# Retention and MoE layer on eight cores: which PSUM banks hold the hoisted LayerNorm sums, and how the GroupNorm broadcasts take turns on theirs

## What is computed

```python
# retention, on xn = layernorm(x)
q, k, v = xh @ wq, xh @ wk, xh @ wv            # per head, 16 heads of 64
scores = einsum('bsnd,btnd->bnst', q, k) * D   # D: causal decay gamma_n^(s-t)
ret = einsum('bnst,btnd->bsnd', scores, v)
mean, var = ret.mean(-1), ret.var(-1)          # per token and head: GroupNorm
norm = (ret - mean) / sqrt(var + 1e-05)
norm = norm.reshape(b, s, h) * gn_scale + gn_bias
gate = xn @ w1
x = x + (gate * sigmoid(gate) + norm) @ w2
# then x = x + moe(layernorm(x)): 8 experts, top 2, and a shared expert
```

## Time and profile before

| | |
|---|---|
| time, median of 2 runs | 1908.31 us (1904.4 to 1912.22) |
| the profiled execution's own time | 1912.23 us |
| its span on the slowest core, core 2 | 1910.7 us |
| spans of the eight cores | 1886.9 to 1910.7 us |
| mean granted TensorE clock of the cores | 0.839 to 0.844 |
| busy on core 2: PE, DVE, ACT | 1534.9, 812.7, 378.4 us |
| GroupNorm statistics of block 0 begin (L823) | 169.20 us into the span |
| the same for block 3 | 642.30 us into the span |

### The profile page before, as it was taken

The page is one execution under the profiler, slowest core; times in us unless marked ns, Lnnn a source line. Parts: engine busy times, 40 slices in busy tenths (PEclk is TensorE's granted clock), DMA queues, the critical chain, the costliest instruction groups (busy, mean ns, idle before and its releaser), DMA issues.

```text
span 1910.7 us, 20876 instructions; the slowest of 8 cores (1886.9 to 1910.7 us)
## 1 busy us (share of the span) xinstructions
PE 1534.9 (80%) x7156; PEld 617.3 (32%) x7156; DVE 812.7 (43%) x1534; ACT 378.4 (20%) x683; POOL 25.0 (1%) x34
## 2 busy tenths in 40 slices
PE   0665776777677558998998999999999999999960
PEld 0221222122121123443443434444444444444420
DVE  0376577577656742222233233332333333332333
ACT  2423322342241121101221111111112111111100
POOL 1000000000000000000000000000000000000000
PEclk9755755765585568999999999999999999999985
DMA  9000020020000053004103222022221302223015
GB/s 147 4 1 1 0 45 1 0 45 1 1 23 1 0 96 59 1 1 59 30 10 43 38 45 45 1 45 44 45 44 20 69 1 45 45 45 67 1 66 176
DMA packets 41352, 67.26 MB, mean 35 GB/s; under 512 B 3858, under 2 KB 16530, under 8 KB 41250
## 3 DMA queue, kind: packets, MB, share of 16 engines
q0 software_dynamic: 26432, 48.65, 16.3%
q1 hardware_dynamic: 14818, 17.29, 2.8%
HBM read 101.96 MB, written 12.58 MB: 60 GB/s over the span
## 4 chain that ended last, share of the span: by engine, by line
PE 64%; DMA 14%; DVE 11%; issue 4%; DVEq 4%; ACT 2%; POOL 0%; ACTq 0%; SPq 0%; POOLq 0%
PE P L1255 20%; PE P L1287 18%; DMA we_sb<-we 10%; PE P L666 3%; PE P L1120 3%; PE P L1131 3%; PE P L1173 3%; PE P L713 3%; PE P L916 3%; PE P L451 3%; DMA xj<-x 2%; DVEq L97 2%; DVE s_sb L697 2%; DMA x1rl<-x1s 2%; DVEq L883 1%
## 5 line engine op out<-in xcount | busy, mean ns | idle before, releaser
L1255 PE MATMUL P<-x2st,we_sb 128*128 128x512 bf16 x2048 | 455.1, 384 | 11.6 <-DMA we_sb<-we 11.6
L1287 PE MATMUL P<-htil,we_sb 128*128 128x512 bf16 x1984 | 438.3, 382 | 12.4 <-DMA we_sb<-we 12.3
L1266 ACT ACTIVATE hs_scr<-P 128x512 bf16<-128x512 f32 x256 | 152.9, 597 | 780.2 <-PE P L1255 779.0
L1255 PEld LDWEIGHTS P<-x2st,we_sb 128*128 128x128 bf16 x2048 | 199.7, 99 | 259.1 <-issue 29.4
L1299 DVE TENSOR_TENSOR acc<-acc,P 128x512 f32<-128x512 f32 x248 | 170.6, 688 | 260.8 <-PE P L1287 260.8
L1287 PEld LDWEIGHTS P<-htil,we_sb 128*128 128x128 bf16 x1984 | 194.8, 98 | 251.9 <-issue 22.4
L1273 DVE TENSOR_TENSOR htil<-hs_scr,bcomb 128x512 bf16<-128x512 bf16 x256 | 108.9, 425 | 357.7 <-ACT hs_scr L1266 357.7
L713 PE MATMUL P<-s_sb,vst 128*64 128x512 bf16 (+3 forms) x128 | 58.2, 455 | 49.4 <-DVE s_sb L697 49.3
L451 PE MATMUL P<-xlnj,w1a_sb 128*128 128x512 bf16 x256 | 66.5, 419 | 28.9 <-DVE xlnj L391 26.4
L690 DVE SCALAR_TENSOR_TENSOR s_sb<-P,gmn_sb,masks_sb 128x512 bf16<-128x512 f32 (+3 forms) x128 | 70.1, 548 | 37.2 <-PE P L672 36.4
L666 PE MATMUL P<-qt,kst 64*128 64x512 bf16 x128 | 73.4, 585 | 13.8 <-DVE ktok L598 6.7
(11 more groups left out here) (167 smaller groups left out, 1257.8 us busy)
## 6 DMA issues: line engine op xcount, KB each, us to landing
we_sb<-we POOLq DMA_DIRECT2D x16, 2048.0 KB, 15.0
out<-acc SPq DMA_DIRECT2D x4, 2048.0 KB, 7.9
xj<-x POOLq DMA_DIRECT2D x4, 1024.0 KB, 25.0
x1s<-xj SPq DMA_DIRECT2D x4, 1024.0 KB, 5.1
wgu_sb<-wgu POOLq DMA_DIRECT2D x1, 4096.0 KB, 31.7
x1rl<-x1s SPq DMA_DIRECT2D x4, 1024.0 KB, 10.4
w1a_sb<-w1a POOLq DMA_DIRECT2D x1, 2048.0 KB, 20.6
w2a_sb<-w2a POOLq DMA_DIRECT2D x1, 2048.0 KB, 32.6
```

Source lines behind the costliest of these rows:

```text
L1255: last = e.matmul(bank[:, :], we1_sb[:, 1024 * k + 128 * f:1024 * k + 128 * f + 128], x2st[:, ST * k + 512 * j:ST * k + 512 * j + 512], st ...
L1266: e.activation(hs_scr[:, hsl:hsl + 512], bank[:, :], AF.Silu),
L1287: last = e.matmul(bank[:, :], we2_sb[:, 1024 * f + 128 * m:1024 * f + 128 * m + 128], htil[:, pslot + 512 * f:pslot + 512 * f + 512], star ...
```

## The change

Five edits at the end of a block, none in the arithmetic. (1) `ln_partA` of the next block gets P[0] and P[1] for its sums in place of P[4] and P[5], and its first matmul waits for the last score evictions of that pair and the last q and k evictions in place of `m_retj_ev[7]`. (2) Since these banks are also the first broadcast pair, gnb of c = 0 now waits for `hoist_fin` and `ln1_ctx[3]`. (3) The first omk01 no longer waits for these two. (4) The broadcast pairs go by `gnb_pair`: pair 0 (P[0], P[1]) for c = 0 alone, then pairs 1 and 2 in turn, so that from c = 3 on gnb of c waits for gapply of c - 2. (5) The LayerNorm broadcast at the end waits for `m_om[0]`, the last user of P[0] and P[1], in place of `m_om[6]`.

```diff
--- before.py
+++ after.py
@@ -843,14 +843,16 @@
 
                 hoist_fin = None
                 if j + 1 < nj:
-                    ln1_ctx = ln_partA(m_x_next, P[4], P[5],
+                    ln1_ctx = ln_partA(m_x_next, P[0], P[1],
                                        xoff=4096 * ((j + 1) % 2),
                                        bufs=(ln1_f, ln1scr, ln1_b),
-                                       first_waits=[m_retj_ev[7]])
+                                       first_waits=list(prev_sev[0] or ()) +
+                                                   list(m_qkev[7]))
                     hoist_fin = ln1_ctx[1]
 
                 m_om = [None] * 8
-                prev_gnb = [None, None, None]
+                gnb_pair = [0, 1, 2, 1, 2, 1, 2, 1]
+                prev_gnb = {0: None, 1: None, 2: None}
                 prev_op = [m_retj_ev[7], m_retj_ev[7]]
                 def omk01(m, k, extra=()):
                     def omk(e, m=m, k=k, xlo=xlo):
@@ -863,16 +865,20 @@
                                 waits=[m_w2a, m_om[k]] + list(extra),
                                 mark=(k == 7))
                 for c in range(8):
-                    bA = (P[0], P[2], P[6])[c % 3]
-                    bB = (P[1], P[3], P[7])[c % 3]
+                    pid = gnb_pair[c]
+                    bA = (P[0], P[2], P[6])[pid]
+                    bB = (P[1], P[3], P[7])[pid]
                     def gnb(e, c=c, bA=bA, bB=bB):
                         e.matmul(bA[:, :], selb_sb[0:16, 128 * c:128 * c + 128],
                                  stat_b[0:16, 0:512], start=True, stop=True)
                         return e.matmul(bB[:, :], selb_sb[0:16, 128 * c:128 * c + 128],
                                         stat_b[0:16, 512:1024], start=True, stop=True)
                     m_b = p.do("tensor", gnb,
-                               waits=[m_gfin, m_selb, prev_gnb[c % 3]] +
+                               waits=[m_gfin, m_selb, prev_gnb[pid]] +
                                      ([m_ktevA_last] if c == 2 else []) +
+                                     ([hoist_fin,
+                                       ln1_ctx[3] if j + 1 < nj else None]
+                                      if c == 0 else []) +
                                      list(prev_sev[0] or ()) +
                                      list(prev_sev[1] or ()), mark=True)
                     def gapply(e, c=c, bA=bA, bB=bB, xlo=xlo):
@@ -891,14 +897,12 @@
                                             gatej[:, 512 * c:512 * c + 512])
                     m_om[c] = p.do("vector", gapply,
                                    waits=[m_b, m_gate[c], m_gns, m_gnb], mark=True)
-                    prev_gnb[c % 3] = m_om[c]
+                    prev_gnb[pid] = m_om[c]
                     if c >= 3:
-                        omk01(0, c - 3, extra=([prev_op[0], hoist_fin]
-                                               if c == 3 else []))
-                        omk01(1, c - 3,
-                              extra=([prev_op[1]] +
-                                     ([ln1_ctx[3]] if j + 1 < nj else [])
-                                     if c == 3 else []))
+                        omk01(0, c - 3, extra=([prev_op[0]] if c == 3
+                                               else []))
+                        omk01(1, c - 3, extra=([prev_op[1]] if c == 3
+                                               else []))
 
                 if STAGE < 6:
                     break
@@ -959,7 +963,7 @@
                 if j + 1 < nj:
                     ln1_next = ln_partB(ln1_ctx, P[0], P[1],
                                         ("ln1", 4096 * ((j + 1) % 2)),
-                                        bc_waits=[m_om[6]])
+                                        bc_waits=[m_om[0]])
 
                 if STAGE < 7:
                     break
```

## The result

The changed kernel takes 1922.74 us, the median of 13 runs, against 1905.52 us of 12 runs of before; the ratio is 1.009, with a 95% interval of 1.0058 to 1.0121. Two later measurements of the same kernel gave 1.0079 (1.0046 to 1.0111) and 1.0055 (1.0033 to 1.0077). So it is slower, by 0.5 to 0.9%. The forecast was 1917.6 us, in a range of 1908 to 1926.

A forecast was written before the change was run, and what follows sets the result against it. The block end was taken as serial: LayerNorm sums, DVE's eight applications, PE's projection. Three blocks at 3.1 us gave 9.3 us, added to the 1908.3 us median of two runs: 1917.6 us, range 1908 to 1926.

The forecast's parts named there:

- Edit 2: Ends of blocks 0 to 2: first broadcast waits for `hoist_fin`, first application 2.9 to 3.3 us later, 3.1 taken per block.
- Edits 1, 3 and 5: Other banks for the sums and L354's wait for `m_om[0]`: 0 us each; the dropped omk01 wait got no separate term.
- Edit 4: Broadcast rotation at all four block ends: two pairs cost 0 us, with 0.6 us of slack left at half clock.
- Rival C: Broadcast rotation on PE becomes the limit with two pairs: 25 us over four blocks, some 1943 us in all; chance 0.03.
- Rival A: Block ends: delay absorbed because something else held PE's projection; no longer than before, 1908 us or 1906; chance 0.10.
- Rival B: LayerNorm sums start early, tail hides beside the GroupNorm statistics: at most 20 us faster in three blocks, 1888 us; chance 0.03.
- Rival D: Stage behind PE's longer pause runs at half clock to its end: 26 us in three blocks, some 1944 us; chance 0.03.

The follow-up runs named there:

- the shorter chain: Changed kernel with ACT copying the mean out right behind L335, first broadcast waiting only for that copy and L338; ratio 0.9969 (0.9915 to 1.0022), attention stretch 475.75 us.

## Why the prediction was right, step by step

- **Edit 2, the term of the sum.** The mechanism was as forecast: the first broadcast is released by L346, PE idle before it 3.69 us (forecast 3.6), and nothing covers the delay. Its size in the sum was 3.1 us a block; over blocks 0 to 2 of the eight cores the start of the first application moved by 4.02 - 0.60 = 3.42 us. Two things were mis-sized. First, I took the middle between the clocks, where the half clock held in 22 of the 24 block ends: 0.2 us. Second, the hop from L346's end to the broadcast was 187.78 - 187.52 = 0.26 us in every block end, where the earlier trace rows had 0.15: 0.1 us. From the broadcast to DVE blocks 1 and 2 had the 1.11 us of the row; block 0 had 1.25 us at half clock on six cores and 0.83 at full clock on two, 1.15 on average. By the stretch of three block ends the change costs 10.3 us, against 9.3 in the sum and 9.9 at its upper end.
- **Edits 1, 3 and 5, nothing.** The kernel with new banks and no wait has the time of before (1.0002), and the changed kernel needs the same time as before from the last application to the next block's statistics.
- **Edit 4, nothing.** The rotation alone has the time of before (1.0003), and DVE's idle time didn't grow. The applications kept their rhythm, block 3 included. Rival C (two pairs too few) is out.
- **Rival A, absorbed.** Out: the whole of the delay shows in the stretch, and 1.0 us more in the tail gave 0.9 us more per block.
- **Rival B, the sums start early.** It didn't happen in the changed kernel, for the reason given: the squares stayed behind the square root on ACT. It did happen once they were moved, with 3.3 to 3.4 us a block gained (473.1 to 463.0 and 463.4 us over three). That the banks had a part in this gain is not shown, since the old ones were free in time too.
- **Rival D, the clock.** The projection had the same 5 us at half clock as before. The pause did bring the clock down, as the Trainium skill (TensorE: Matmul & The Clock Gate, HAM oscillation) describes for gaps. The trace agrees in 22 of 24 block ends, but at this place it lengthens only the time to the first application.
- **The total.** 1922.74 us is 5 us above the forecast and inside the range. It lies so near in part by luck, since two errors offset each other: the forecast stood on 1908.3 us of two runs, and 12 runs of before gave 1905.5; the measured difference is 17.2 us, where the sum had 9.3. The first two totals were 17 and 15 us over before (1.009, 1.0079), the third 10.5 us (1.0055). The block ends are equally long in all three (483.4 to 483.7 us), and behind the last application of block 3 the profiles give 1228.5, 1228.2 and 1225.4 us on average, against 1227.3 before. So I hold the surplus of the first two for spread of the part behind the block ends; that is argued from these numbers, not shown by an experiment of its own, and the interval of the first total begins above 1.0054.

## What to carry to other kernels

When work is hoisted into a spare bank, what counts is who uses that bank next: here the next user was the head of the critical chain, where before it had been a matmul with slack. A wait that costs nothing at one place in an engine's list can cost the rest of its chain when it stands eight matmuls earlier. And before banks are moved, it is worth reading whether the old ones were what the work waited for: here they had been free for over 9 us, and what held the sums was the order of ACT's list. With the new banks and no wait the time stayed as it was (1.0002); with the sums listed 7.5 us earlier as well it fell by 0.6% in one measurement (0.9942), and by an unclear 0.35% (0.9965) in the other.

## What I had not expected

The granted clock didn't follow the length of the pause alone. Behind a pause of 3.69 us the first pair ran at half clock in 22 of 24 block ends of the changed kernel's first profile; in block 0 of cores 4 and 7 it ran at full clock. Behind a pause of 1.6 us it began at full clock in block 0 on all eight cores, but nearly all of it at half on three cores in block 1. With the early sums it ran at half clock behind 2.74 us on core 2, where the last sums had still run at full clock (0.38 us each). From the first broadcast to the application the half clock costs 0.42 us in every block: 1.25 against 0.83 us in block 0, and 1.11 against 0.69 us in blocks 1 and 2.

The wait of the first broadcast on ACT took 0.26 us from the end of the ACT row to the start of the matmul; with the shorter chain, where DVE released the same instruction, it took 0.15 us, as the wait of L354 on ACT did in the earlier trace rows. In block 0 the application also follows the end of the pair later, by 0.24 us (188.16 + 0.63 = 188.79 to 189.03), where blocks 1 and 2 have 0.1 us (353.38 + 0.63 = 354.01 to 354.12). What makes these differences stays open.
